# Two-layer graph attention: weighting gathered neighbour rows on ScalarE, summing a batch of them with one VectorE reduction, and another order of the work around it

## The chip, the cores and the metric

One Trainium2 chip, of which the kernel uses one core. The metric is the device time of one execution in microseconds (us): the median over several runs. A smaller number is better.

## What is computed

The input is `x`, 8192 nodes by 256 features, and `adj`, an 8192 x 8192 matrix of 0 and 1 with about 0.1% of ones (symmetric, with ones on the diagonal). Two attention layers, each added to its input:

```python
def reference(x, adj, L0_gnn_W, L0_gnn_a, L1_gnn_a):
    h = jnp.maximum(_layernorm(x, axis=-1), 0.0)
    x = x + _L0_gnn_ref(h, adj, L0_gnn_W, L0_gnn_a)   # softmax over neighbours of e_left + e_right, times h @ W, leaky relu
    h = jnp.maximum(_layernorm(x, axis=-1), 0.0)
    x = x + _L1_gnn_ref(h, adj, L1_gnn_a)
    return x

def _L1_gnn_ref(h, adj, a):
    h1, h2 = h @ a[:d], h @ a[d:]
    e = jax.nn.leaky_relu(h1 + h2.T, negative_slope=0.01)
    attention = softmax(jnp.where(adj > 0, e, NEG_BIG), axis=1)
    return attention @ h
```

## The kernel before

The kernel runs layer 0 first, as dense matmuls over all 64 tiles of 128 nodes. During it, each node's list of neighbours is decoded, and the nodes of the last 44 tiles are sorted by their number of neighbours. The change touches layer 1 alone, which is the second block of the program (from about 1066 us of the profile on). Layer 1 works on the nodes in two ways at once.

**The dense part** does 20 tiles on TensorE. It goes in NGD = 5 groups of G = 4 tiles, and each group in NC = 16 *chunks* of CB = 4 blocks of 128 keys, so there are C = 80 chunks, numbered n. A chunk is 4 blocks x 4 tiles x 2 parts (positive and negative sum, `Vp` and `Vn`) x 2 halves (a high and a low float16 half of each value) = 64 matmuls of 128x128 on 257 columns (L1639). Chunk n needs two masks:
- ScalarE's `signs` (L1300): four activations of 128x512 write which scores are negative, into one of two buffers `adjn`. For the first or second half of chunk n+1 they wait until TensorE is through that half of chunk n-1 (`unit_used`).
- VectorE's `unpack` (L1456, L1459, every second chunk) spreads adjacency bits into `adjp`; `negatives` (L1473) ands it with the signs, `positives` (L1478) xors. After `positives` TensorE may start the chunk (`pos_ready`).

In the first group (chunks 0 to 15) the values themselves have to be made as well: for each of the 64 key tiles SyncE loads a row tile into one of four `hs` buffers, ScalarE makes the high halves (`high_halves`, L1289, 8 per chunk), VectorE the low halves (`low_halves`, L1438, 8 per chunk), and the buffer is free again. At the end of a group VectorE's `take_sums` and ScalarE's `scale_sums` read the eight PSUM banks, `add_negatives` joins the two sums, and the result is stored.

**The sparse part** does the other 44 tiles by gathering. A tile m of 128 nodes has `slots[m]` neighbour slots (24 for the first tile, 4 for the last, 420 in all, worked out by `slot_counts`). GpSimd issues one indirect DMA for each slot (L1264): 128 rows of 258 float32 from `h_of_layer1` into a buffer `gat`. Slots go in 88 *batches* of 3 to 6 (`BS` = 6 at most; tiles of over 6 slots take several), in a ring of `NBUF` = 4 batch buffers. GpSimd may start batch k when VectorE is through all rows of batch k-4 (L1262). For a batch, ScalarE's `weights(k)` makes two small exponentials `e8` (L1321) and VectorE's `larger(k)` their maximum `w8` (L1515). Then VectorE's `add_row` multiplies a row by its weight and adds it to a running sum in `sacc`: L1531 for a tile's first two slots, L1534 for all others. `join`, `divide` and `add_x1` (L1539, L1544, L1550) finish a tile, 128 x1 rows for it come by a DMA that ScalarE issues (`load_rows`), and GpSimd scatters the finished tile to the output (L1255), five batches later at the earliest.

The order on each engine is written out by hand, per chunk n. `pace` says how many rows are to be added by each chunk: none in the first three (`HEAD` = 3.0), then 7 per chunk in the first group and 5 or 6 per chunk (5.3 on average) in the others. Worked out from the code, the numbers for the chunks are 0, 0, 0, 5, 7, 7, ... and 88 rows by the end of chunk 15. On VectorE rows are dealt out between `unpack`, `negatives`, `positives` and the low halves:

```python
add_rows(q0, cuts[0])            # 1 row
negatives(n, g, c)
add_rows(cuts[0], cuts[1])       # 2 rows
positives(n, c)
if g == 0:
    for j in range(CB):
        low_halves(c * CB + j, j % HS)
add_rows(cuts[1], q1)            # the rest
```

On ScalarE the order in a chunk is: high halves of chunk n, `weights` of the batches that begin up to 3 rows (`LEAD`) past the rows of this chunk, `scale_sums` if a group has ended, and then the signs of chunk n+1.

## Time and profile before

| | |
|---|---|
| median of 3 runs | 1924.2 us (1916.23 to 1925.32) |
| profiled execution, its own time | 1914.35 us |
| its span, first to last instruction | 1912.5 us |
| mean granted TensorE clock | 0.930 of full speed |
| busy share of the span: PE, PEld, DVE, ACT, POOL | 88%, 73%, 63%, 51%, 34% |

All times in the text are on the clock of the profiled execution, from the start of its span. PE is TensorE's matmuls, PEld its weight loads, DVE VectorE, ACT ScalarE, POOL GpSimd, SP SyncE. The busy share of PE overstates it, since matmuls overlap: one is recorded as 270 ns or more, while they follow each other every 111 ns at full clock. Counts of matmuls in a stretch of time therefore say more than busy time. A TensorE clock of 1.00 is 2.4 GHz, 0.50 is 1.2 GHz.

### The profile page before, as it was taken

The numbers are of one execution on the slowest core, as the hardware profiler recorded it, in microseconds if no ns is written. First come the engines' busy times: TensorE is split into PE (matmuls) and PEld (weight loads), VectorE is DVE, ScalarE is ACT, GpSimd is POOL, SyncE is SP. The second block draws the span as 40 slices with busy tenths as digits, with TensorE's granted clock in tenths as the row PEclk, the third lists the DMA queues.
The fourth block names the chain that finished last, engine by engine and source line by source line (L and its number), as shares of the span: only waits on it lengthen the run. The fifth ranks groups of instructions, "written<-read, shape, count | busy, mean of one in ns | idle before, by whom it ended". The sixth has DMA issues, their size and how long they took to land. (4 is left out here: it accounts for less than half of the span.)

```text
span 1912.5 us, 37724 instructions
## 1 busy us (share of the span) xinstructions
PE 1691.5 (88%) x13955; PEld 1391.3 (73%) x13955; DVE 1203.0 (63%) x4595; ACT 973.4 (51%) x1367; POOL 651.6 (34%) x607
## 2 busy tenths in 40 slices
PE   6888999999999999999999397677888888978878
PEld 5646888888888888888888285454666667757657
DVE  7488888988888888674444377652435445435434
ACT  5987665665666556666662375432333233323322
POOL 0000000000000000026665548755656657665562
PEclk9998999999999999999999698877889889979889
DMA  8529998888988889989994534533333333433331
GB/s 287 182 76 386 342 349 325 314 311 321 354 320 326 318 310 331 355 333 378 386 379 104 130 94 134 160 80 88 101 89 83 111 89 94 117 100 99 88 92 52
DMA packets 142801, 410.60 MB, mean 215 GB/s; under 512 B 26193, under 2 KB 90066, under 8 KB 109906
## 3 DMA queue, kind: packets, MB, share of 16 engines
q1 hardware_dynamic: 108434, 329.85, 47.6%
q0 software_dynamic: 27904, 73.43, 13.9%
q10 hardware_dynamic: 6336, 5.77, 1.0%
q8 instruction: 62, 1.02, 0.2%
q14 instruction: 65, 0.53, 0.1%
HBM read 368.94 MB, written 40.03 MB: 214 GB/s over the span
## 5 line engine op out<-in xcount | busy, mean ns | idle before, releaser
L984 PE MATMUL banks<-HV,adjT 128*128 128x257 f16 x8192 | 938.8, 274 | 16.7 <-DVE adjT L658 8.8
L984 PEld LDWEIGHTS banks<-HV,adjT 128*128 128x128 fp8e4 x8192 | 792.5, 98 | 148.2 <-DVE HV L688 23.7
L1639 PE MATMUL banks<-Vp,adjp 128*128 128x257 f16 x2560 | 540.6, 292 | 115.4 <-issue 59.2
L1639 PE MATMUL banks<-Vn,adjn 128*128 128x257 f16 x2560 | 538.1, 291 | 48.9 <-issue 47.7
L1264 POOL DMA_INDIRECT gat<-h_of_layer,rec x420 | 465.8, 1109 | 275.5 <-issue 117.9
L444 ACT ACTIVATE adj_f<-adj_i 128x2048 fp8e4<-128x2048 int32 x256 | 480.1, 1898 | 6.6 <-DMA adj_i<-in_adj 6.5
L1300 ACT ACTIVATE adjn<-h1bc,nh 128x512 fp8e5<-128x512 f32 x320 | 212.1, 716 | 446.2 <-remote 272.1
L1639 PEld LDWEIGHTS banks<-Vp,adjp 128*128 128x128 fp8e4 x2560 | 261.2, 103 | 192.3 <-issue 126.5
L1639 PEld LDWEIGHTS banks<-Vn,adjn 128*128 128x128 fp8e4 x2560 | 262.2, 103 | 124.8 <-issue 76.5
L425 POOL DMA_DIRECT2D HV<-x_after_layer x44 | 25.5, 580 | 773.4 <-DVE rank L911 741.3
L1473 DVE TENSOR_TENSOR adjn<-adjp,adjn 128x1024 uint16<-128x1024 uint16 x80 | 55.4, 692 | 334.8 <-ACT adjn L1300 296.0
L1534 DVE SCALAR_TENSOR_TENSOR sacc<-gat,w,sacc 128x257 f32<-128x257 f32 x332 | 152.5, 477 | 0.0
L492 ACT ACTIVATE pk<-banks 128x512 uint16<-128x512 uint16 x64 | 37.9, 593 | 170.3 <-PE banks L969 143.9
L695 DVE RECIPROCAL rden<-banks 128x1 f32<-128x1 f32 x64 | 10.7, 168 | 145.9 <-PE banks L984 115.3
L655 DVE TENSOR_SCALAR adjT<-pk 128x512 uint16<-128x512 uint16 x448 | 94.6, 282 | 0.0
L957 PE MATMUL banks<-w_sb,hT 128*128 128x257 f32 x256 | 68.9, 392 | 15.6 <-ACT hT L456 15.3
L627 DVE SCALAR_TENSOR_TENSOR fold<-adj_f 128x1024 int32<-128x1024 int32 x64 | 77.2, 1206 | 7.4 <-ACT adj_f L444 7.4
L418 POOL DMA_INDIRECT x_after_layer_sorted<-HV,rank x44 | 66.5, 1512 | 13.4 <-issue 12.2
L525 ACT ACTIVATE hh<-x,nmr,rstd 128x256 f32<-128x256 f32 x64 | 38.4, 601 | 53.6 <-DVE nmr L727 45.8
L1515 DVE TENSOR_TENSOR w<-e 128x5 f32<-128x5 f32 (+2 forms) x88 | 13.9, 157 | 77.8 <-ACT e L1321 58.5
L519 ACT ACTIVATE std<-mv,eps 128x1 f32<-128x1 f32 x64 | 18.8, 294 | 86.0 <-DVE mv L719 83.9
L1255 POOL DMA_INDIRECT out<-sout,rec x44 | 46.5, 1058 | 43.1 <-DVE sout L1550 31.8
(158 smaller groups left out, 1395.2 us busy)
## 6 DMA issues: line engine op xcount, KB each, us to landing
adj_i<-in_adj SPq DMA_DIRECT2D x256, 1024.0 KB
h_of_layer<-hh SPq DMA_DIRECT2D x64, 129.0 KB
hs<-h_of_layer SPq DMA_DIRECT2D x64, 129.0 KB
xt<-in_x SPq DMA_DIRECT2D x64, 128.0 KB
packed_adj<-pk SPq DMA_DIRECT2D x64, 128.0 KB
x_after_layer<-x SPq DMA_DIRECT2D x64, 128.0 KB
HV<-in_x SPq DMA_DIRECT2D x14, 512.0 KB, 8.8
gat<-h_of_layer,rec POOLq DMA_INDIRECT x420
```

Of the source, the lines that this page charges most:

```text
L418: pool.indirect_dma_start(x1s_d, bass.IndirectOffsetOnAxis(ap=rank[:, m:m + 1], axis=0), HV[:, T + m % SH, 0:D], None).then_inc(xs_out[m % ...
L444: nc.scalar.activation(adj_f[:, b, q * QC:(q + 1) * QC], adj_i[:, q, :], ACT.Copy, scale=2.0, saturate=False).then_inc(conv_done, 1)
L627: nc.vector.scalar_tensor_tensor(four, whole[:, 0:4 * GW], 1, whole[:, 4 * GW:8 * GW], ALU.logical_shift_right, ALU.bitwise_or)\
L655: last = nc.vector.tensor_scalar(adjT[:, b, i, :], pk[:, pb, :], PAIR << i, 6 - i, ALU.bitwise_and, ALU.logical_shift_left)
L957: last = nc.tensor.matmul(wps[t % 3][:, 0:DV], hT[:, t % 2, c, :], w_sb[:, c, :], start=(c == 0), stop=(c == 1))
L984: last = nc.tensor.matmul(acc[b][:, 0:DV], adjT_h[:, b, i, q, :, h], V0[:, jb, s, 0:DV], start=(jb == 0 and s == 0), stop=(jb == T - 1 and ...
L1255: pool.indirect_dma_start(out, bass.IndirectOffsetOnAxis(ap=rec[:, m, OWN:OWN + 1], axis=0), sout[:, m % NOUT, :], None).then_inc(so_out[m ...
L1264: pool.indirect_dma_start(gat[:, k % NBUF, s - s0, :], None, h_d, bass.IndirectOffsetOnAxis(ap=rec[:, m, s:s + 1], axis=0))\
L1300: i = nc.scalar.activation(adjn_b[:, c % 2, jb // 2, :, jb % 2], h1bc[:, g2, :], ACT.Relu, scale=-BIG, bias=nh2[:, tiles[j]:tiles[j] + 1], ...
L1473: nc.vector.tensor_tensor(part, both, part, ALU.bitwise_and).then_inc(neg_ready, 1)
L1534: nc.vector.scalar_tensor_tensor(acc, x, w, acc, ALU.mult, ALU.add)\
L1639: mm = nc.tensor.matmul(bank[2 * i + part][:, 0:DV], m[:, i * P:(i + 1) * P], V[:, j, s, 0:DV], start=(j == 0 and s == 0), stop=(j == T - ...
```

## The change

Rows of a batch are no longer multiplied and added one by one on VectorE. ScalarE's new `scale_rows(k)` multiplies each row of batch k by its weight in place (one activation of 128x257 per slot), and VectorE's new `sum_rows(k)` sums all of them with one reduction over the slot axis. If a tile has several batches, the sum of one is written into a spare seventh slot of the next batch's buffer and is summed there with the rest. `join` is gone, and `sacc` holds one sum for a tile instead of two.

The steps of a batch are spread over three chunks: for the batches `taken(n)`, `weights` is on ScalarE in chunk n, `larger` on VectorE and `scale_rows` on ScalarE in chunk n+1, `sum_rows` on VectorE in chunk n+2, and `divide` and `add_x1` in the chunk after it. A batch's buffer is handed back to GpSimd after `sum_rows`. `load_rows` is issued by `scale_rows` at a tile's first batch.

In a chunk ScalarE makes the signs of the next chunk first and then does `scale_rows`, the high halves of chunk n+2, and `weights`. VectorE does `negatives` and `positives` next to each other, then `take_sums` where a group has ended, the low halves of chunk n+1, `sum_rows`, `unpack` for the next chunk, and `larger`. The halves of chunk 0, and the high halves of chunk 1, are made ahead of the loop.

The pace is another: worked out from the new constants, one batch is taken in chunk 0 already, 19 batches by the end of chunk 15, then about one per chunk (5.0 rows), 86 of the 88 by the end of chunk 79 (in four chunks none, in ten of them two). The last two batches, of 5 and 4 rows, come behind the last group's `take_sums` and `add_negatives`.

```diff
@@ -1034,8 +1034,9 @@
         BS = 6
         NBUF = 4
         LEAD = 3
-        FIRST = 1.35
-        HEAD = 3.0
+        FIRST = 1.13
+        HEAD = -2.0
+        TAIL = 1.4
         OUT_LAG = 5
         NOUT = 4
 
@@ -1045,28 +1046,16 @@
             parts = -(-slots[m] // BS)
             for i in range(parts):
                 batch.append((m, slots[m] * i // parts, slots[m] * (i + 1) // parts))
...
         at = [sum(slots[:m]) for m in range(NS + 1)]
         last = [max(k for k in range(len(batch)) if batch[k][0] == m) for m in range(NS)]
         fills = [sum(batch[i][2] - batch[i][1] for i in range(k % NBUF, k + 1, NBUF)) for k in range(len(batch))]
         pace = [max(0.0, FIRST * min(n, NC) + max(0, n - NC) - HEAD) for n in range(C)]
...
+        rows_in = [at[NS] * a / (pace[-1] + TAIL) for a in pace]
+        weighed = [0] + [sum(1 for m, s0, s1 in batch if at[m] + s1 <= a) for a in rows_in]
+
+        def taken(n):
+
+            return range(weighed[n], weighed[n + 1]) if n >= 0 else range(0)
...
-            gat = sb("gat", [P, NBUF, BS, ROW], f32)
-            sacc = sb("sacc", [P, 2, 2, DV], f32)
+            gat = sb("gat", [P, NBUF, BS + 1, ROW], f32)
+            sacc = sb("sacc", [P, 2, DV], f32)
...
-            sacc_ready = sem("sacc_ready")
-            row_added = sem("row_added")
+            scaled = sem("scaled")
+            summed = sem("summed")
...
-                        pool.wait_ge(row_added, begin[k - NBUF + 1])
+                        pool.wait_ge(summed, k - NBUF + 1)
...
+                def scale_rows(k):
+
+                    m, s0, s1 = batch[k]
+                    if s0 == 0:
+                        load_rows(m)
+                    act.wait_ge(w8_ready, k + 1)
+                    for i in range(s1 - s0):
+                        x = gat[:, k % NBUF, i, 0:DV]
+                        made = nc.scalar.activation(x, x, ACT.Copy, scale=w8[:, k % 2, i:i + 1])
+                    made.then_inc(scaled, 1)
+
...
-                for m in range(NOUT - 2):
-                    load_rows(m)
+                def high_chunk(c):
+                    for j in range(CB):
+                        high_halves(c * CB + j, j % HS, (c * CB + j) // HS * 16 + 16)
+
+                high_chunk(0)
                 act.wait_ge(nh2_ready, 1)
                 act.wait_ge(h1bc_in[0], 16)
-                act.wait_ge(hb_ready, 2)
                 for h in range(2):
                     signs(h, 0, 0, 0, h, False)
-                weighed = out_done = 0
+                high_chunk(1)
+                act.wait_ge(hb_ready, 2)
                 for n in range(C):
                     g, c = n // NC, n % NC
...
-                    for m in range(out_done, ended(rows_by[n])):
-                        if m + NOUT - 2 < NS:
-                            load_rows(m + NOUT - 2)
-                        out_done = m + 1
-                    for k in range(weighed, lead_of(rows_by[n + 1])):
-                        weights(k)
-                        weighed = k + 1
-                    for m in range(out_done, awaited(rows_by[n + 1])):
-                        if m + NOUT - 2 < NS:
-                            load_rows(m + NOUT - 2)
-                        out_done = m + 1
                     if g > 0 and c == 0:
                         scale_sums(g - 1, g == 1)
                     if n + 1 < C:
@@ -1359,9 +1348,18 @@
                             act.wait_ge(h1bc_in[g1 % 2], 16 * (g1 // 2 + 1))
                         for h in range(2):
                             signs(2 * n + 2 + h, n + 1, g1 % 2, c1, h, 2 * n + 2 + h >= RB)
-                for m in range(out_done + NOUT - 2, NS):
-                    load_rows(m)
+                    for k in taken(n - 1):
+                        scale_rows(k)
+                    if n + 2 < NC:
+                        high_chunk(n + 2)
+                    for k in taken(n):
+                        weights(k)
+                for k in taken(C - 1):
+                    scale_rows(k)
                 scale_sums(NGD - 1, NGD == 1)
+                for k in range(weighed[C], len(batch)):
+                    weights(k)
+                    scale_rows(k)
...
@@ -1511,85 +1509,94 @@
                     b = batch[k][2] - batch[k][1]
                     dve.wait_ge(e8_ready, 2 * k + 2)
                     if k >= 2:
-                        dve.wait_ge(row_added, begin[k - 1])
+                        dve.wait_ge(scaled, k - 1)
                     nc.vector.tensor_tensor(w8[:, k % 2, 0:b], e8[:, k % 2, 0, 0:b], e8[:, k % 2, 1, 0:b],
                                             ALU.max).then_inc(w8_ready, 1)
 
-                def add_row(q):
-
-
-                    m, s, k = row[q]
-                    i = s - batch[k][1]
-                    acc = sacc[:, m % 2, s % 2, :]
-                    if i == 0:
-                        dve.wait_ge(w8_ready, k + 1)
-                    x = gat[:, k % NBUF, i, 0:DV]
-                    w = w8[:, k % 2, i:i + 1]
-                    if s < 2:
-                        if m >= 2 and s == 0:
+                def sum_rows(k):
+
+
+                    m, s0, s1 = batch[k]
+                    b = s1 - s0
+                    dve.wait_ge(scaled, k + 1)
+                    if s0:
+                        dve.wait_ge(summed, k)
+                    if k == last[m]:
+                        if m >= 2:
                             dve.wait_ge(so_ready, m - 1)
-                        nc.vector.tensor_scalar(acc, x, w, None, ALU.mult).then_inc(row_added, 1)
+                        to = sacc[:, m % 2, :]
                     else:
-                        dve.wait_ge(row_added, q - 1)
-                        nc.vector.scalar_tensor_tensor(acc, x, w, acc, ALU.mult, ALU.add)\
-                            .then_inc(row_added, 1)
-
-                def join(m):
-                    dve.wait_ge(row_added, at[m + 1])
-                    nc.vector.tensor_tensor(sacc[:, m % 2, 0, :], sacc[:, m % 2, 0, :], sacc[:, m % 2, 1, :],
-                                            ALU.add).then_inc(sacc_ready, 1)
+                        to = gat[:, (k + 1) % NBUF, batch[k + 1][2] - batch[k + 1][1], 0:DV]
+                    nc.vector.reduce_sum(to, gat[:, k % NBUF, 0:b + (1 if s0 else 0), 0:DV]
+                                         .rearrange("p s c -> p c s"), AX.X).then_inc(summed, 1)
 
                 def divide(m):
-                    dve.wait_ge(sacc_ready, m + 1)
-                    nc.vector.reciprocal(srd[:, m % 2:m % 2 + 1], sacc[:, m % 2, 0, D:DV])\
+                    dve.wait_ge(summed, last[m] + 1)
+                    nc.vector.reciprocal(srd[:, m % 2:m % 2 + 1], sacc[:, m % 2, D:DV])\
                         .then_inc(srd_ready, 1)
 
                 def add_x1(m):
                     dve.wait_ge(srd_ready, m + 1)
                     dve.wait_ge(x1s_in[m % NOUT], 16 * (m // NOUT + 1))
-                    nc.vector.scalar_tensor_tensor(sout[:, m % NOUT, :], sacc[:, m % 2, 0, 0:D],
+                    nc.vector.scalar_tensor_tensor(sout[:, m % NOUT, :], sacc[:, m % 2, 0:D],
                                                    srd[:, m % 2:m % 2 + 1], sout[:, m % NOUT, :],
                                                    ALU.mult, ALU.add).then_inc(so_ready, 1)
 
-                def add_rows(q0, q1):
-
-                    for q in range(q0, q1):
-                        m, s, k = row[q]
-                        for b in range(lead_of(q) if q else 0, lead_of(q + 1)):
-                            larger(b)
-                        add_row(q)
-                        if m and s == 2:
-                            join(m - 1)
-                        if m and s == 3:
-                            divide(m - 1)
-                        if m and s == min(4, slots[m] - 1):
-                            add_x1(m - 1)
-                    if q1 == len(row) and q0 < q1:
-                        join(NS - 1)
-                        divide(NS - 1)
-                        add_x1(NS - 1)
-
+                def low_chunk(c):
+                    for j in range(CB):
+                        low_halves(c * CB + j, j % HS)
+
+                unpack(0, 0, 0, False)
+                low_chunk(0)
                 dve.wait_ge(ab_ready, 1)
+                closing = []
                 for n in range(C):
                     g, c = n // NC, n % NC
-                    q0, q1 = rows_by[n], rows_by[n + 1]
-                    cuts = (min(q0 + 1, q1), min(q0 + 3, q1))
-                    if c % UB == 0:
-                        unpack(n, g, c, n >= 2 * UB)
-                    add_rows(q0, cuts[0])
                     negatives(n, g, c)
-                    add_rows(cuts[0], cuts[1])
                     positives(n, c)
-                    if g == 0:
-                        for j in range(CB):
-                            low_halves(c * CB + j, j % HS)
-                    add_rows(cuts[1], q1)
                     if g > 0 and c == 0:
                         take_sums(g - 1)
+                    for m in closing:
+                        divide(m)
+                    if n + 1 < NC:
+                        low_chunk(n + 1)
+                    for m in closing:
+                        add_x1(m)
+                    closing = []
+                    for k in taken(n - 2):
+                        sum_rows(k)
+                        closing += [m for m in range(NS) if last[m] == k]
+                    if n + 1 < C and (n + 1) % UB == 0:
+                        unpack(n + 1, (n + 1) // NC, (n + 1) % NC, n + 1 >= 2 * UB)
                     if g > 0 and c == 1:
                         add_negatives(g - 1)
+                    for k in taken(n - 1):
+                        larger(k)
+                for m in closing:
+                    divide(m)
+                    add_x1(m)
+                for k in taken(C - 2):
+                    sum_rows(k)
+                    for m in range(NS):
+                        if last[m] == k:
+                            divide(m)
+                            add_x1(m)
+                for k in taken(C - 1):
+                    larger(k)
+                    sum_rows(k)
+                    for m in range(NS):
+                        if last[m] == k:
+                            divide(m)
+                            add_x1(m)
                 take_sums(NGD - 1)
                 add_negatives(NGD - 1)
+                for k in range(weighed[C], len(batch)):
+                    larger(k)
+                    sum_rows(k)
+                    for m in range(NS):
+                        if last[m] == k:
+                            divide(m)
+                            add_x1(m)
...
```

## Rows read from the trace of the kernel before

**Rows 1.** The page's costliest groups: xcount | busy us, mean ns | idle before, releasers.

```profile
L1639 PE MATMUL banks<-Vp,adjp 128*128 128x257 f16 x2560 | 540.6, 292 | 115.4 <-issue 59.2
L1264 POOL DMA_INDIRECT gat<-h_of_layer,rec x420 | 465.8, 1109 | 275.5 <-issue 117.9
L1300 ACT ACTIVATE adjn<-h1bc,nh 128x512 fp8e5<-128x512 f32 x320 | 212.1, 716 | 446.2 <-remote 272.1
L1534 DVE SCALAR_TENSOR_TENSOR sacc<-gat,w,sacc 128x257 f32<-128x257 f32 x332 | 152.5, 477 | 0.0
```

**Rows 2.** Stretches: us; busy (x) of PE, PEld, DVE, ACT, POOL; clock, DMA share, GB/s.

```profile
1081.90:1104.10 22.20, 11.93 (x64) 7.83 (x65) 7.73 (x20) 8.23 (x19) 13.10 (x13) 0.65 0.78 130
...
1140.80:1219.70 78.90, 60.33 (x449) 47.69 (x450) 55.21 (x150) 43.78 (x102) 64.51 (x48) 0.85 0.48 132
1219.70:1271.10 51.40, 28.01 (x193) 19.68 (x194) 27.05 (x79) 16.64 (x41) 29.07 (x29) 0.75 0.43 124
...
1320.00:1868.20 548.20, 466.74 (x3586) 362.51 (x3584) 242.80 (x709) 176.73 (x360) 335.10 (x314) 0.88 0.35 96
1868.20:1903.80 35.60, 35.60 (x322) 30.88 (x319) 17.64 (x50) 10.51 (x20) 7.81 (x8) 1.00 0.16 49
```

**Rows 3.** Shorter stretches, cut where GpSimd's runs of gathers begin, last on or end.

```profile
1403.00:1411.80 8.80, 8.80 (x81) 7.39 (x79) 4.69 (x14) 2.55 (x6) 6.96 (x7) 1.00 0.39 106
1411.80:1418.60 6.80, 3.62 (x26) 2.24 (x24) 0.00 (x0) 0.50 (x1) 5.26 (x6) 1.00 0.49 136
...
1482.80:1490.70 7.90, 7.90 (x65) 6.51 (x64) 3.31 (x12) 2.94 (x6) 6.38 (x6) 0.87 0.59 173
...
1567.50:1589.80 22.30, 22.30 (x203) 19.46 (x202) 12.43 (x37) 7.83 (x16) 18.00 (x15) 1.00 0.43 120
...
1287.50:1315.90 28.40, 14.46 (x59) 5.58 (x57) 4.83 (x15) 3.06 (x6) 22.00 (x22) 0.61 0.38 100
```

**Rows 4.** The waits: who waited for whom, us in total, times, longest.

```profile
POOL gat L1264 <- DVE sacc L1534: 115.8, 25, 22.9
POOL gat L1264 <- DVE sacc L1531: 41.8, 10, 14.7
...
ACT e L1321 <- DMA gat<-h_of_layer,rec: 37.9, 9, 10.9
```

**Rows 5.** The timeline: start us, us, instruction, [idle before <- releaser].

```profile
1123.19 0.48 DVE L1438 SCALAR_TENSOR_TENSOR Vp<-hs,Es,Vp 128x258 f16<-128x258 f32 x1
1123.59 0.48 DVE L1438 SCALAR_TENSOR_TENSOR Vn<-hs,Es,Vn 128x258 f16<-128x258 f32 x1
...
1124.39 3.28 POOL L1264 DMA_INDIRECT gat<-h_of_layer,rec  x1 [0.30 <-issue]
...
1412.63 0.95 POOL L1264 DMA_INDIRECT gat<-h_of_layer,rec  x1 [0.30 <-issue]
```

**Rows 6.** Groups by line, of the operations that the change removes, adds or moves.

```profile
L1289 ACT ACTIVATE Vp<-hs,Es 128x258 f16<-128x258 f32 x64 | 31.8, 497 | 2.7 <-DMA hs<-h_of_layer 2.7
L1438 DVE SCALAR_TENSOR_TENSOR Vp<-hs,Es,Vp 128x258 f16<-128x258 f32 x64 | 30.6, 479 | 0.0
L1531 DVE TENSOR_SCALAR sacc<-gat,w 128x257 f32<-128x257 f32 x88 | 30.3, 353 | 0.5 <-DVE w L1515 0.3
...
L1386 DVE TENSOR_REDUCE red_in<-h2all 128x1 f32<-128x64 f32 x1 | 0.2, 207 | 0.0
...
L1389 DVE TENSOR_REDUCE red_in<-x1g 128x1 f32<-128x44 f32 x1 | 0.2, 188 | 0.0
...
L905 DVE TENSOR_REDUCE rsum<-HV 128x44 f32<-128x880 f32 x1 | 1.8, 1771 | 0.0
...
L525 ACT ACTIVATE hh<-x,nmr,rstd 128x256 f32<-128x256 f32 x64 | 38.4, 601 | 53.6 <-DVE nmr L727 45.8 <-issue 7.7
```

**Rows 7.** The timeline of the end.

```profile
1896.02 0.96 POOL L1255 DMA_INDIRECT out<-sout,rec  x1 [2.08 <-DVE sout L1550]
...
1906.42 1.42 DVE L1505 TENSOR_TENSOR x1g<-x1g,hs 128x256 f32<-128x256 f32 x4
```

15 lines of the change are left out of this document (removed).

## The prediction, made before the changed kernel was run

> **What bounds the kernel now.** I read the page first, then the waits, then layer 1 cut into stretches, and last the timeline of GpSimd beside that of TensorE. The change is in layer 1, so only the time from the first matmul of L1639 at 1081.9 us to the last at 1903.8 us can move, and what hangs behind it. The page names TensorE as the busy engine, but 292 ns for one matmul is an overlapped figure [rows 1]. The last stretch gives the true rate: 322 matmuls in 35.6 us at full clock, 0.111 us each, or 7.1 us for a chunk of 64 [rows 2]. Eighty chunks would be 568 us, and they take 821.9 us. The 254 us above that floor are the subject.
>
> I get the number of chunks of a stretch by dividing its matmuls by 64 [rows 2]. Chunk 0 takes 22.2 us. Chunks 1 to 5 fill the 36.7 us up to the next row and are at the floor. Chunks 6 to 12 take 78.9 us, 11.3 each. Chunks 13 to 15 take 51.4 us. Chunks 16 to 18 fill the 48.9 us from 1271.1 to 1320.0. Chunks 19 to 74 take 548.2 us, 9.8 each, and the last five 7.1 each. The excesses are 15, 1, 29, 30, 28 and 152 us.
>
> Two different causes are behind them. In chunks 6 to 12 the sparse part sets the pace. ScalarE has `weights` ahead of the signs of the next chunk and waits there for gathers, 37.9 us in nine waits [rows 4]; TensorE then waits for masks. GpSimd was left idle for 22.9 us before this, the longest wait for L1534 [rows 4], because no row is added before chunk 3.
>
> The other cause costs more. Look at a run of gathers [rows 3]. From 1403.0 to 1411.8 us GpSimd issues 7 operations and TensorE does 81 matmuls, full rate. From 1411.8 to 1418.6 us, with GpSimd still issuing, TensorE does 26, or 3.8 per us instead of 9. VectorE does nothing and ScalarE almost nothing there, so TensorE is not held by masks; the page puts its idle time down to "issue" [rows 1]. The worst case has 59 matmuls in 28.4 us beside 22 operations of GpSimd, 22 us lost. A short run, 6 operations from 1482.8 us, leaves TensorE at full rate within the counts. So TensorE loses its supply some 9 us into an unbroken run of gathers and regains it when the run ends. Why, no row says. GpSimd's runs end when its four buffers are full: 157.6 us of waits for VectorE [rows 4]. One gather every 0.95 + 0.30 = 1.25 us [rows 5] and some 5.6 issues per chunk, 314 in 56 chunks [rows 2], are 7.0 us against a floor of 7.1. At full rate GpSimd therefore never pauses, TensorE starves, and the pause comes out of TensorE's time.
>
> **Part one: ScalarE multiplies.** 420 activations of 128x257. The nearest rows are L1289 at 497 ns and L525, which reads and writes float32, at 601 ns [rows 6]. Consecutive ones overlap; L1438 on VectorE, recorded at 0.48 us, starts every 0.40 us [rows 5], and I take 0.40 us for ScalarE too (0.50 as the upper end). Five slots are 2.0 us per chunk. Four signs (716 ns each) [rows 1] are under 2.9 us and the small exponentials 0.6 us. This is 5.5 us of a chunk of 7.1 us or more, behind the signs, so from chunk 16 on it costs nothing. If that cover goes, it is up to 2.5 us per chunk.
>
> **Part two: VectorE sums.** It loses 30.3 + 152.5 us [rows 6, 1] and 44 joins. It gains 88 reductions over 420 slots and 44 carried sums, 464 x 257 = 119,248 elements. L905 reduces across a stride, as the new one does: 1771 ns for 880 elements, 2.01 ns each. The contiguous L1386 and L1389 differ by 19 ns for 20 elements, 0.95 ns each, with some 0.15 us fixed. The ends are 126 and 240 us; I take 240, since only L905 is strided. A batch of 5 takes 2.6 us. VectorE then has 1.4 (masks) + 2.9 + under 1.5 us for the rest, below 7.1; this costs nothing outside the first group and the end.
>
> The Trainium skill (SBUF — State Buffer, section "Door 1: The DMA port swizzle") says that consecutive accesses pay when each leaves a 16-byte line, which a step of 1032 bytes always does. It agrees with L905 against the contiguous pair; by it the reductions are 240 us, without it 126 us, and the forecast moves by the 3 us at the end alone.
>
> **Part three: the first group.** Chunk 0 stays: 24 gathers run from the start as before, so TensorE starves as before until about 1104 us. Then a loop forms between ScalarE and VectorE. From the end D of a VectorE chunk, where `larger` is, ScalarE scales (2.4 us), then makes 8 high halves; VectorE can start the low halves at D + 3.0 and needs 8 x 0.40 = 3.2 us for them, then 1.2 batches of reductions (3.4 us), then half an unpack, `larger` and a closing, 0.6 us. That is 10 us per chunk (8.4 with cheap reductions). GpSimd needs about the same: 5.9 operations at 1.25 us, and one of them is stretched to 3.28 us by the block of low halves [rows 5], in all 9.7 us. VectorE starts chunk 2 at about 1106 us; twelve chunks of 10 and two of 8 us put the start of chunk 16 at about 1245 us instead of 1271, a gain of 26 us. But of the 51.4 us of chunks 13 to 15, 22 us are a starvation that could come again. I give it one half and take 15 us. The starvation in chunk 18 (22 us) was as long because GpSimd, three batches behind, could go on without a pause. In the new order three batches sit in the pipeline, and GpSimd can only be about one ahead; I halve this one too: 11 us.
>
> **Part four: chunks 19 to 74.** Signs first and a gather's wait behind them: no gain, since masks come in time here already. What may change is GpSimd's share. Its 335.1 us of busy time and 314 gaps of 0.30 us are 429 us, 1.37 us per operation instead of 1.25 [rows 2, 5]: operations stretch beside VectorE's two-input operations. Without 420 row operations I take 1.29 us, 0.4 us less per chunk: 22 us. The bounds are nothing and 95 us (every chunk at 8.1 us, if each buffer handed back singly gives a pause).
>
> The Trainium skill (SBUF — State Buffer, "Who interferes with whom") has it that a VectorE instruction with two SBUF inputs contends with GpSimd's reads and that a reduction never contends. The trace agrees as far as the 3.28 us gather under the low halves goes; a block of reductions beside gathers is in no row.
>
> **Part five: the end.** The last five chunks were free of gathers and ran at 7.1 us; now gathers go on to chunk 78, at 9.4 us each: 11 us lost. After the last matmul the old order ends with L1505 at 1907.8 us and a store, 4.7 us more [rows 7]. The new one then has two batches in series: `larger` 0.15, scaling 2.1, sum 2.6, closing 0.6, then 0.15, 1.7, 2.1 and 0.6 us, a scatter of 0.96 us and its landing. This ends about 1922 us against 1912.5; with cheap reductions 1919. I take 9 us lost. Moving `load_rows` (44 DMAs on ScalarE's queue) behind the signs costs nothing unless its wait for a scatter bites; GpSimd issues this after the batch that follows. It could add 1 or 2 us in each of the last six tiles.
>
> **The sum.** -15 - 11 - 22 + 11 + 9 = -28 us. From the profiled execution's own 1914.4 us (span 1912.5) that gives 1886 us. This execution lies 10 us under the median of the three runs; on the median, 1924 - 28 = 1896 us.
>
> **Rivals.**
> *A, the forecast:* shorter first group, slightly shorter middle, longer end; 1870 to 1912 us. Chance 0.44.
> *B, the pauses cure the starvation.* VectorE hands back one buffer at one point of a chunk. If even 1 us of pause is enough (the short run speaks for it) [rows 3], chunks 19 to 79 take 8.1 to 8.5 us: 80 to 100 us gained there, less 9 at the end, 15 from the first group: about 1820 us. Against it: buffers came back about one per chunk before as well. Chance 0.15.
> *C, the supply is conserved.* If every gather costs TensorE a fixed number of matmuls wherever it stands, 464 issues cost the same, and only idle masks in the first group are saved, 12 us, against 9 at the end: 1921 us. For it: 254 us over 464 issues is 0.55 us each, and neither number changes. Chance 0.20.
> *D, slower: gathers come faster and starve TensorE more.* One mechanism: VectorE's row operations slow GpSimd down, and where they do TensorE keeps its rate: 15 operations in 22.3 us, 1.5 us each, and 203 matmuls, without loss [rows 3]. Without them every run goes at 1.25 us and starves TensorE from its ninth us. With 0.5 us more lost per chunk in 61 chunks this is +30 us, and with the end's 9, the first group's gain of 15: about 1948 us. It decides from 0.3 us more per chunk on. Chance 0.21.
>
> **How the numbers follow.** The likeliest is A, 1896 us. The median's own runs spread by 0.5%, and under that nothing can be told from no change. A gives faster but for a sliver (0.41), B faster (0.15), C mostly the same (0.18), D slower: 0.58 faster, 0.20 the same, 0.22 slower. A's own range is 1870 to 1912 us. For 8 in 10 I leave out the far side of B and D's tail: 1830 to 1945 us.
>
> **What would show it.** In the new profile: reductions of 2.6 us for 5 slots (1.4 would be the cheap price); the start of chunk 16 near 1245 us; runs of GpSimd that are rarely over two batches; chunks of the middle near 9.4 us; scaling activations starting every 0.40 us; 14 us or more from the last matmul to the end. The prediction is wrong if TensorE starves in short runs as well, if ScalarE waits in `load_rows` or for `larger` and the signs come late, or if chunks of the first group take over 11 us.

## The result, and the profile after

The changed kernel took 1991.7 us (median of 4 runs, 1987.3 to 2001.3) against 1924.8 us (4 runs, 1916.2 to 1933.8): 1.0354 times the time, interval 1.0309 to 1.0398. It is slower, and outside the range of the forecast.

The page of the profile after, the costliest groups that answer to [rows 1, 6]:

```profile
L1646 PE MATMUL banks<-Vp,adjp 128*128 128x257 f16 x2560 | 546.5, 293 | 142.9 <-issue 83.0
L1253 POOL DMA_INDIRECT gat<-h_of_layer,rec x420 | 421.8, 1004 | 417.5 <-DVE gat L1530 159.7
```

The new operations, by line and shape:

```profile
L1321 ACT ACTIVATE gat<-gat,w 128x257 f32<-128x257 f32 x420 | 175.6, 496 | 36.1 <-DVE w L1513 28.7
```
```profile
L1530 DVE TENSOR_REDUCE gat<-gat 128x257 f32<-128x1285 f32 x14 | 34.0, 2431 | 0.7 <-ACT gat L1321 0.6
L1530 DVE TENSOR_REDUCE gat<-gat 128x257 f32<-128x771 f32 x5 | 5.1, 1028 | 0.0
```

A gather became 105 ns shorter (1109 to 1004 ns), yet GpSimd's idle time before gathers grew from 275.5 to 417.5 us, and TensorE's idle time put down to "issue" before this half of its matmuls from 59.2 [rows 1] to 83.0 us. The waits of the kernel after, which answer to [rows 4]:

```profile
PEld banks L1646 <- issue: 283.8, 284, 15.7
...
POOL gat L1253 <- DVE gat L1530: 159.7, 25, 18.0
...
POOL gat L1253 <- DVE sacc L1530: 129.0, 20, 18.6
```

GpSimd now waits 288.7 us in 45 waits for a buffer to be handed back, where it was 157.6 us in 35. ScalarE's wait for gathers fell from 37.9 to 7.4 us, as meant. The stretches of layer 1, with columns as in [rows 2]: first group, the four other groups, the end:

```profile
1083.00:1262.20 179.20, 134.08 (x1024) 105.19 (x1025) 126.08 (x232) 129.42 (x305) 98.03 (x94) 0.86 0.48 124
1262.20:1969.20 707.00, 553.89 (x4096) 416.56 (x4096) 327.31 (x511) 327.31 (x727) 354.14 (x358) 0.84 0.30 84
1969.20:1992.40 23.20, 0.24 (x3) 0.00 (x0) 9.55 (x21) 6.14 (x17) 1.92 (x2) 0.57 0.15 48
```

The kernel before, cut at the same points (start of chunk 16, last matmul):

```profile
1271.10:1903.60 632.50, 535.82 (x4096) 413.65 (x4096) 276.46 (x806) 198.45 (x403) 377.99 (x355) 0.87 0.34 93
```

So the first matmul comes 1 us later, the first group is 10 us shorter (179 for 189), the 64 chunks of groups 1 to 4 take 74.5 us more (707.0 for 632.5, 11.0 us a chunk for 9.9), and the end 14 us more (23.2 for 8.9): 80 us, the difference of the spans 1992.4 and 1912.5. The place is the middle. There I took every pair of matmuls whose starts lie more than 0.35 us apart, and summed what each such gap has beyond the usual 0.11 us: 202 us in 228 gaps after, 131 us in 165 before. So 71 of the 74.5 us are such gaps. None of them ends with a mask that came late: 193 us of the 202 are put down to "issue" or to nothing (120 of the 131 before), the rest to the sums of a finished group being taken out of the banks.

One of them, cut where GpSimd's run of gathers begins, where TensorE falls, where it recovers and where the next run begins:

```profile
1568.70:1576.40 7.70, 7.70 (x72) 6.69 (x70) 5.09 (x8) 3.72 (x9) 5.82 (x7) 1.00 0.32 88
1576.40:1584.40 8.00, 3.46 (x16) 1.41 (x14) 0.00 (x0) 1.34 (x2) 4.77 (x5) 0.72 0.37 98
1584.40:1590.80 6.40, 6.39 (x48) 5.17 (x48) 4.68 (x7) 4.95 (x11) 0.04 (x1) 0.82 0.08 24
1590.80:1597.10 6.30, 6.30 (x59) 5.50 (x58) 4.10 (x7) 4.13 (x10) 5.07 (x5) 1.00 0.45 125
1598.20:1606.50 8.30, 6.85 (x59) 5.19 (x56) 4.60 (x7) 4.49 (x11) 5.24 (x6) 1.00 0.48 128
```

The reader is to see the fall from 72 matmuls in 7.7 us to 16 in 8.0, with VectorE at nothing and ScalarE nearly so, and GpSimd at work for the first 6 us of it. The run had 11 operations. The recovery is not at full rate at once: the granted clock is 0.82 of the upper level (2.4 GHz) after TensorE idled, and 48 matmuls take 6.4 us. A run of five operations from 1590.8 us, behind a pause of 8.4 us, costs nothing. The next one, also of five and behind a pause of 1.1 us (last row), costs 2 us.

Counted over groups 1 to 4, with a run ended by any pause over 0.6 us: before, the 11 runs of up to six operations cost nothing. After, there are 17 such runs. The ten behind a pause of over 2 us cost nothing, and of the seven behind a shorter one six cost something, 13.5 us together. In runs of nine operations or more the first gap comes at a median of 8.0 us from the run's start, where it was 10.4 us before. The runs of seven or more cost 0.64 us of such gaps for each operation of GpSimd (179 us, 280 operations), where it was 0.34 (97 us, 282 operations).

Not only new matmuls are late. ScalarE's signs wait for TensorE to be through half a chunk, and the page can't name what released 251.8 us of these waits ("remote"). From the records of the instructions: of 124 such halves in groups 1 to 4, ScalarE, idle, began its signs over 1 us after TensorE's last matmul of the half in 41, up to 18.5 us after it. The end of the first group shows it on VectorE, whose `take_sums` waits for the last matmul of the group alone:

```profile
ACT adjn L1289 <- remote: 251.8, 41, 19.6
```
```profile
1250.27 0.39 PE L1646 MATMUL banks<-Vn,adjn 128*128 128x257 f16 x2
...
1260.63 0.16 DVE L1480 TENSOR_TENSOR cnt<-idf,banks 128x8 f32<-128x8 f32 x1 [12.92 <-remote]
```

Ten us lie between the two, and GpSimd's run of gathers ends at 1258.5 us, in between. VectorE, in contrast, follows ScalarE's signs within 0.5 us in all 64 chunks. So during a long run two things come late, TensorE's next matmuls and the word that those already started are done. A matmul that has started isn't waiting for its instruction, so a theory of the cause has to explain more than a lack of those.

### The profile page after: what moved, and what is told of

It reads as the page before. It is cut to its first block and busy times, and to the rows that moved or that the text cites. A ratio compares the mean times of both kernels' runs of the same rounds, so it can differ in the third digit from the quotient of the medians.

```text
span 1992.4 us, 37734 instructions
## 1 busy us (share of the span) xinstructions
PE 1707.7 (86%) x13955; PEld 1393.4 (70%) x13955; DVE 1268.8 (64%) x4219; ACT 1139.8 (57%) x1787; POOL 598.5 (30%) x607
## 5 line engine op out<-in xcount | busy, mean ns | idle before, releaser
L1646 PE MATMUL banks<-Vp,adjp 128*128 128x257 f16 x2560 | 546.5, 293 | 142.9 <-issue 83.0
L1646 PE MATMUL banks<-Vn,adjn 128*128 128x257 f16 x2560 | 544.8, 293 | 70.8 <-issue 69.5
L1253 POOL DMA_INDIRECT gat<-h_of_layer,rec x420 | 421.8, 1004 | 417.5 <-DVE gat L1530 159.7
L1289 ACT ACTIVATE adjn<-h1bc,nh 128x512 fp8e5<-128x512 f32 x320 | 211.0, 715 | 359.3 <-remote 251.8
L1321 ACT ACTIVATE gat<-gat,w 128x257 f32<-128x257 f32 x420 | 175.6, 496 | 36.1 <-DVE w L1513 28.7
L1530 DVE TENSOR_REDUCE sacc<-gat 128x257 f32<-128x1542 f32 (+3 forms) x44 | 128.4, 2918 | 24.5 <-ACT gat L1321 18.6
L1530 DVE TENSOR_REDUCE gat<-gat 128x257 f32<-128x1028 f32 (+4 forms) x44 | 98.5, 2238 | 2.9 <-ACT gat L1321 2.4
L957 PEld LDWEIGHTS banks<-w_sb,hT 128*128 128x128 f32 x256 | 45.3, 197 | 23.4 <-ACT hT L456 19.6
```

Of the source, the lines that this page charges most:

```text
L957: last = nc.tensor.matmul(wps[t % 3][:, 0:DV], hT[:, t % 2, c, :], w_sb[:, c, :], start=(c == 0), stop=(c == 1))
L1253: pool.indirect_dma_start(gat[:, k % NBUF, s - s0, :], None, h_d, bass.IndirectOffsetOnAxis(ap=rec[:, m, s:s + 1], axis=0))\
L1289: i = nc.scalar.activation(adjn_b[:, c % 2, jb // 2, :, jb % 2], h1bc[:, g2, :], ACT.Relu, scale=-BIG, bias=nh2[:, tiles[j]:tiles[j] + 1], ...
L1321: made = nc.scalar.activation(x, x, ACT.Copy, scale=w8[:, k % 2, i:i + 1])
L1530: nc.vector.reduce_sum(to, gat[:, k % NBUF, 0:b + (1 if s0 else 0), 0:DV] .rearrange("p s c -> p c s"), AX.X).then_inc(summed, 1)
L1646: mm = nc.tensor.matmul(bank[2 * i + part][:, 0:DV], m[:, i * P:(i + 1) * P], V[:, j, s, 0:DV], start=(j == 0 and s == 0), stop=(j == T - ...
```

## The same kernel in two conditions

The experiments ran in five more sessions, each with the kernel before beside them. In one its median was 1933.7 us (13 runs, 1921.6 to 1942.3), close to the result's 1924.8. In the other four it was 1754.9, 1753.6, 1753.4 and 1758.5 us. The difference sits in layer 1: its first matmul starts at 1081.9 us in the one trace of this kernel and at 1082.6 in the other. A session kept its condition through all its runs, and one chip showed both. What chooses the condition no row says, and I could not bring it about; it stays open. I call the 1930 us condition *starved* and the other *supplied*. Times I compare only inside a session. For stretches of traces that isn't possible everywhere, since the starved kernel before has its one trace in the session of the result; where two sessions are compared, the text says so.

The kernel before itself, one execution in the supplied condition, over groups 1 to 4 and over 20 us of them:

> The kernel before, unaltered, for a profile beside the two others. Where TensorE isn't starved (near 1754 us): GpSimd without idle time from chunk 3 on and TensorE waiting for masks behind it, 3 to 4 us after the gathers' pace; a change that frees GpSimd of VectorE's two-input operations then gains. Where it is: the same stretches as in the first profile, within 2%.

```profile
1241.30:1738.70 497.40, 464.82 (x4095) 399.03 (x4096) 280.44 (x806) 198.56 (x403) 377.23 (x356) 0.98 0.42 119
```
```profile
1400.00:1420.00 20.00, 20.00 (x183) 17.46 (x181) 12.27 (x37) 8.47 (x18) 15.43 (x16) 1.00 0.58 173
```

It took 1749.3 us. Sixteen operations of GpSimd in 20 us without a pause leave TensorE at 183 matmuls, the full rate. GpSimd is the bound here: beyond the 0.30 us between two operations it is idle for 13 us in 497, ScalarE waits 252.2 us for gathers instead of 37.9 [rows 4], and the chain that ended last has gathers for 20% of the span. The same gathers go with a starved TensorE in one condition and not in the other: no gap of over 0.35 us between matmuls is put down to "issue" here, and ScalarE's signs begin over 1 us after TensorE's half once in 124 halves, 1.6 us late.

The page's queue of instructions is the same in both conditions, the changed kernel starved and the kernel before supplied:

```profile
q8 instruction: 62, 1.02, 0.2%
```

Its transfers in layer 1, 48 in each trace, take 1.05 us on the mean in both. Once under way they are not slower. Whether they are asked for or begun late no row says, but the short loop below settles that they are not the cause.

## The experiments

Three theories stood. *Rival D* (theory 1 in the texts on record): gathers no longer slowed by VectorE's two-input operations starve TensorE more. *The new order and pace* (theory 2): one hand-back point per chunk, three batches in a pipeline of four buffers, so that GpSimd's pauses fall badly, whoever does the arithmetic. *Code*: TensorE's loop over a group is unrolled, and its instructions come too late. Against all of them stood the conserved supply (C).

**Starved session** (kernel before 1933.7 us). First the changed kernel unaltered.

> The changed kernel, unaltered, as a control: the kernel before ran at 1754.9 us on the chip of the first four experiments, against 1924.8 us where the change was measured, and its changed form was not among them. If this chip is like that one (before near 1755 us): theory 1 (the loss of the change is starvation of TensorE beside gathers, which that chip does not show) expects 1735 to 1745 us, faster than before; theory 2 (order and pace cost by themselves) expects over 1800 us. If this chip is like the one of the result (before near 1925 us): 1985 to 2000 us.

1995.6 us (4 runs, 1981.9 to 2017.6; without the longest the median is 1993.5), ratio 1.028 (1.022 to 1.034). The slowdown repeats; groups 1 to 4 took 704.9 us, 0.3% from the result's trace.

**Row arithmetic back on VectorE,** in the new order and at the new pace:

```
-                    act.wait_ge(w8_ready, k + 1)
-                    for i in range(s1 - s0):
-                        x = gat[:, k % NBUF, i, 0:DV]
-                        made = nc.scalar.activation(x, x, ACT.Copy, scale=w8[:, k % 2, i:i + 1])
-                    made.then_inc(scaled, 1)
...
-                    nc.vector.reduce_sum(to, gat[:, k % NBUF, 0:b + (1 if s0 else 0), 0:DV]
-                                         .rearrange("p s c -> p c s"), AX.X).then_inc(summed, 1)
...
+                            nc.vector.scalar_tensor_tensor(acc, x, w, acc, ALU.mult, ALU.add)\
+                                .then_inc(row_added, 1)
```

> The changed kernel's order and pace with the row operations back on VectorE. On a chip like that of the result, theory 1 expects 1915 to 1945 us and gathers of 1.1 us on average, theory 2 1975 to 2000 us. On a chip like that of the first experiments: 1730 to 1742 us again.

1936.4 us (10 runs, 1926.6 to 1957.1), ratio 1.001 (0.998 to 1.005). First group, and groups 1 to 4:

```profile
1082.10:1231.40 149.30, 124.96 (x1024) 101.64 (x1025) 113.24 (x300) 94.22 (x216) 110.47 (x84) 0.92 0.55 139
1231.40:1925.20 693.80, 554.47 (x4095) 418.87 (x4096) 291.61 (x809) 199.76 (x404) 383.86 (x367) 0.84 0.32 87
```

This is where theory 1 had put it (1915 to 1945 us, gathers of 1.1 us; a gather took 1094 ns on the mean), and not theory 2 (1975 to 2000 us). By the medians of the starved session the order and pace alone cost nothing that can be told from zero, and the arithmetic costs 59 us (1995.6 against 1936.4).

The traces say where, with less certainty. From this kernel to the changed one of the same session the arithmetic adds 30 us in the first group (149.3 to 179.4), 11 in groups 1 to 4 and 4 at the end. The order and pace have to be read across two sessions: against the trace of before they shorten the first group by 40 us (189.2 to 149.3), lengthen groups 1 to 4 by 61 (632.5 to 693.8) and the end by 10 (8.9 to 19.1), 32 us in all where the medians have 3. The other 29 us are the choice of executions: the trace of before lay 10 us under its median, this one 10 above its own, and the two sessions' medians of the kernel before differ by 9. Where these lie no trace says. If all of them lay in groups 1 to 4, the order and pace would cost some 32 us there and the arithmetic some 23. So of the loss in that stage 32 to 61 us belong to the order and pace and 11 to 23 to the arithmetic.

The mechanism of rival D is to be seen in these traces. The time per operation of GpSimd, gap included, falls from 1.346 to 1.288 us between the two. The first gap in runs of nine or more comes at a median of 10.7 us with the rows on VectorE, as before the change (10.4), and at 8.0 us with the reductions, in both traces of the changed kernel. The gaps between matmuls grow from 184 to 199 us. What the order and pace add is another thing: a median onset as late as before, and yet 0.50 us of gaps for each operation in runs of seven or more, for 0.34 (0.59 in the changed kernel run beside it).

**Short loop**: TensorE's inner loop runs over 4 chunks, so that the code of a group is 12 chunks long instead of 16 (the value tiles of chunks 0 to 3 are used again in it).

```
+                    chunks(g, False, range(4))
+                    with pe.Fori(1, NC // 4 - 1) as r:
+                        chunks(g, False, range(4), r)
+                    chunks(g, False, range(NC - 4, NC))
```

> The changed kernel with the shorter TensorE program (an inner loop over four chunks in groups 1 to 4, the value tiles of chunks 0 to 3 used in it). On a chip like that of the result: under 1940 us if TensorE starves for its own instructions, 1980 to 2000 us if for something else. On a chip like that of the first experiments: within 3 us of the changed kernel, since nothing starves there.

1996.9 us (4 runs, 1990.6 to 2011.5), ratio 1.032 (1.026 to 1.038), the same as the changed kernel; gaps between matmuls 200 us. The trace says more than the time. Its instruction queue on the page, and 535 us of it:

```profile
q8 instruction: 30, 0.49, 0.1%
```
```profile
1435.00:1970.00 535.00, 423.06 (x3090) 314.46 (x3089) 249.82 (x404) 247.70 (x557) 270.33 (x272) 0.83 0.30 83
```

The queue moved 30 packets for 62, and in these 535 us none at all (32 in the same 535 us of the changed kernel, with its 16 chunks of code; the page's other queue of instructions, q14, moved 12 in both). Yet 151 us of them are gaps between matmuls. So TensorE starves as much while this queue moves nothing, and late transfers of its code are refuted as the cause.

**Supplied sessions.** These four came first, on one chip (before 1754.9 us): the gathers left out (the buffers are filled once), the rows on VectorE, a filling of 256 float32 on GpSimd awaited behind each gather, and the short loop.

```
+                nc.gpsimd.memset(gat[:, :, :, :], 0.5).then_inc(gat_set, 1)
...
-                        pool.indirect_dma_start(
```
```
+                        nc.gpsimd.memset(idle[:, 0:256], 0.0).then_inc(idled, 1)
+                        pool.wait_ge(idled, at[m] + s + 1)
```

> The changed kernel without its 420 gathers: the gather buffers are filled once with a constant, so the rows of the sparse part are not the reference's; everything else, the 420 scaling activations and 88 reductions among it, stays. Theory 1 (TensorE is starved while gathers run): chunks at 7.1 us from chunk 16 on, no gaps of about 1 us between matmuls, and a time near 1720 us. Theory 3 (ScalarE's and VectorE's new work, or the order of the engines, slows TensorE by itself): gaps and chunks over 9 us stay, and the time stays over 1850 us.

> The changed kernel's order and pace, but a batch's rows are multiplied and added one by one on VectorE as before, in the place of the reduction, and ScalarE's 420 activations are gone. Theory 1 (VectorE's row operations slowed the gathers down and so protected TensorE): gathers are back at a mean of 1.1 us, and the time falls to 1915 to 1945 us. Theory 2 (the order and the pace are the loss: buffers given back in another rhythm, gathers up to the last chunk): the time stays at 1975 to 2000 us.

> The changed kernel with a GpSimd memset of 256 float32 and a wait for its end behind every gather, so that gathers start every 1.6 to 1.8 us instead of every 1.25 us. Theory 1: TensorE starves less; chunks of the middle go to 8.5 to 9.5 us, bounded by GpSimd itself, and the time falls below 1960 us although GpSimd does more. Theory 2: GpSimd has 150 us more to do, and the time rises above 2000 us.

> The changed kernel with a shorter TensorE program: in groups 1 to 4 chunks 4 to 11 are two turns of one inner loop of four chunks, so that a group's code is 12 chunks long instead of 16. In the inner loop the value tiles are those of chunks 0 to 3, so the dense part's sums are not the reference's; the number and shapes of matmuls are the same. If TensorE starves because its own instructions have to be fetched while gathers run, the loss falls in groups 1 to 4, by a third or all of it: under 1940 us. If what starves it is something else (the memory ports, the masks' semaphores), the time stays at 1980 to 2000 us.

They took 1724.1 (ratio 0.983), 1736.7 (0.989, 0.985 to 0.992), 1835.5 (1.047, 1.044 to 1.049) and 1739.2 us (0.992). None can speak on starvation, since there was none to cure. The spaced gathers show only that GpSimd's time is the path here: in groups 1 to 4 it waits 0.8 us for a buffer in all, its other 99 us of idle time are short waits, most of them for the fillings, and the stage takes 548 us where the changed kernel takes 467. Repeated in another session (before 1753.6), the first and the third gave the same, 1723.6 (0.983) and 1835.4 us (1.047):

> The changed kernel without its 420 gathers (constant rows instead, so the sparse part's output is not the reference's), on another chip. If the gathers are the whole difference between the chips: 1724 us as on the first chip, and no gaps between matmuls beyond those at the group ends. If TensorE is starved here by something else as well: over 1750 us.

> The changed kernel with a small memset and a wait for it behind every gather, on another chip. Where TensorE starves: theory B expects less starvation, since gathers are 1.6 us apart instead of 1.25: groups 1 to 4 under 680 us; if only the number of gathers counts, they stay at 706 us or rise, since GpSimd has 150 us more to do. Where nothing starves: 1832 to 1836 us again.

**Depth of the ring**, in the same session: the changed kernel with five buffers (two semaphores of the setup merged to have one more), and the kernel before with three.

```
-        NBUF = 4
+        NBUF = 5
```

> The changed kernel with five gather buffers instead of four. Theory A (a batch now keeps its buffer over three chunks, so GpSimd is stopped for long after every starvation and the depth of the ring is what the new order lacks): groups 1 to 4 fall from 706 us towards 650 us, and the time to 1930 to 1960 us where the kernel before takes 1925 to 1935 us. Theory B (TensorE is starved by the number and the rate of gathers, whatever the ring): within 10 us of 1995 us. Where nothing starves (before near 1755 us) both expect 1735 to 1745 us.

> The kernel before with three gather buffers instead of four. Theory A: slower by 30 us or more, like the new order, because the ring is one buffer shorter. Theory B: within 10 us of the kernel before in groups 1 to 4; the first group may lose some, since GpSimd is the bound there.

1730.5 us (ratio 0.988, 0.985 to 0.990) and 1771.1 us (1.011, 1.008 to 1.013). **The changed kernel** again, with both beside it, in the next session (before 1753.4):

> The changed kernel as it is. Where the kernel before takes near 1755 us: 1735 to 1745 us by theory 1 (the change is faster where TensorE isn't starved). Where it takes near 1930 us: 1985 to 2005 us again.

> The changed kernel with five gather buffers. On a chip that starves TensorE: theory A (the new order lacks ring depth) 1930 to 1960 us; theory B (number and rate of gathers) within 10 us of the changed kernel. On one that doesn't: 1730 us again.

> The kernel before with three gather buffers. On a chip that starves TensorE: theory A slower by 30 us or more, theory B within 10 us in groups 1 to 4. On one that doesn't: 1771 us again.

> The changed kernel without its gathers. On a chip that starves TensorE: 1724 us if the gathers are the whole difference between the chips, over 1750 us if something else starves TensorE too. On one that doesn't: 1724 us.

1740.4 us (5 runs, ratio 0.993, 0.991 to 0.995), 1732.1 (0.989, 0.986 to 0.992), 1770.6 (1.010, 1.007 to 1.014) and 1723.3 us (0.984). The changed kernel's groups 1 to 4, and its last gathers after the last matmul:

```profile
1238.30:1705.10 466.80, 456.80 (x4096) 396.76 (x4096) 322.41 (x505) 323.79 (x725) 352.12 (x353) 1.00 0.45 125
...
1705.10:1740.20 35.10, 0.23 (x3) 0.00 (x0) 15.95 (x28) 8.37 (x23) 12.01 (x13) 0.56 0.26 79
```

The same kernel that is 3% slower in the starved condition is 0.7% faster in this one. Groups 1 to 4 take 467 us for 497 before (one trace each, in sessions that differ by 5 us on the kernel before). GpSimd is the bound, and an operation of it costs 1.299 us for 1.360, which over some 355 operations is 22 of the 30 us; with the rows on VectorE the stage took 483 us, at 1.36 us an operation. The first group gives 6 us, and the end takes 26 back, because 12 operations of GpSimd start after the last matmul. Five buffers are the best kernel that ran, 8 us under the changed one in the same session and 9 us above the one without gathers. A last session (before 1758.5) confirmed it: 1733.3 us (0.986, 0.984 to 0.988) beside 1725.5 us without gathers (0.981).

> The changed kernel with five gather buffers. Where TensorE is starved beside gathers: theory A (the new order lacks ring depth) 1930 to 1960 us; theory B (number and rate of gathers) within 10 us of 1993 us, the changed kernel's time there. Where it isn't: 1731 us again.

> The changed kernel without its gathers. Where TensorE is starved: 1724 us if the gathers are the whole difference, over 1750 us if something else starves TensorE too. Where it isn't: 1724 us.

The five buffers and the kernel without gathers were meant for the starved condition above all, and each session they ran in was supplied. So two things were not tested where they matter: that the starvation goes when the gathers go, and that deeper buffering gives back what the new order costs there.

## Why the prediction was wrong

The step that failed is part four, chunks 19 to 74, and with it the choice of A over D: it took time that GpSimd saves as time that TensorE gets back, -22 us for its 56 chunks. The 64 chunks of groups 1 to 4 took 74.5 us more instead, since TensorE starves by the run, and faster gathers starve it sooner in a run. Point by point:

**Part one, right.** An activation of `scale_rows` is recorded at 496 ns, and five in a row take 2.10 us, so they start every 0.40 us. From chunk 16 on they lie behind the signs.

**Part two, right.** A reduction of 5 slots took 2.43 us (forecast 2.6; the cheap price was 1.4); all 88 take 226.9 us for 119,248 elements, 1.90 ns each (forecast 240 us). The price of L905 holds, with one exception: the five reductions over 3 slots took 1028 ns, 1.33 ns an element at the same stride. The Trainium skill (SBUF — State Buffer, "Door 1: The DMA port swizzle") has it that each access which goes over to a new 16-byte line costs extra. The reductions over 4 to 7 slots, 1.9 to 2.0 ns an element, agree with this; those over 3 slots pay much less, and no run here shows why.

**Part three, the ring right, the starvation not.** Chunks 3 to 14 took 10.5 us each for a forecast 10 (1116.2 to 1241.7 us). But from the start of chunk 15 to that of chunk 16 it took 20.5 us, 11.8 of them the late end of the group shown above, and chunk 17 took 23.3 us: the starvation came again where I had counted half. The start of chunk 16 was forecast at 1245 us from the ring alone and 1256 with the half; it was 1262.2. Of the forecast 15 us, 9 came. The ring between ScalarE and VectorE is dear: with the rows on VectorE the first group is 30 us shorter in the starved condition and 13 us (139.4 for 152.8, two sessions) in the supplied one.

**Part four, wrong in sign.** Its term of 0.4 us less of GpSimd per chunk is exact: an operation with its gap fell from 1.366 to 1.289 us, by 5.6 issues 0.43 us. The Trainium skill's rule behind it (SBUF — State Buffer, "Who interferes with whom") is that a VectorE instruction with two SBUF inputs contends with a GpSimd instruction that reads SBUF, and that a reduction never does. The traces agree with it, in the supplied condition too (1.360 to 1.299 us). But in the starved condition GpSimd's time is not what is paid for. The runs became shorter, the long ones mostly two batches and 13 to 16 us, and cost more: 0.71 us of TensorE for each operation of GpSimd in groups 1 to 4 (707.0 less 64 x 7.1, over 358), against 0.50 before and 0.65 with the rows on VectorE. Runs up to six operations cost nothing behind a long pause (0.6 us at most in the repeat), as the prediction had read from [rows 3], but behind a pause of under 2 us most of them do: its own sign of being wrong, starvation in short runs, came true there. GpSimd's idle time in that stage, beyond the 0.30 us between operations, went 149, 200, 245 us (before, rows on VectorE, after). In place of 9.4 us a chunk stood 11.0. The forecast for groups 1 to 4, 632.5 - 11 - 22 + 11 = 610.5 us, missed by 96 us, and the rest by 12.

**Part five, mis-sized.** The end was forecast 9 us longer and was 14. The timeline of the end has the term that I left out. The last matmul starts at 1969.2 us, and VectorE turns to `larger` here:

```profile
1973.34 0.16 DVE L1513 TENSOR_TENSOR w<-e 128x5 f32<-128x5 f32 x1
```

`larger` of the first of the two batches waits 3.9 us behind the sums of the last group on VectorE (L1480 from 1969.48 us, to L1503). After the last scatter 7.8 us pass to the end of the span; the forecast's terms leave some 7 for that. The two batches in series are as forecast.

**The rivals.** B is refuted: there were more pauses and more starvation, and pauses of 1.1 us did not protect the run behind them. C is refuted too: 462 of the 464 indirect DMAs of GpSimd start before the last matmul, where it was all of them, and it took 80 us more. D has the sign, and its mechanism is there: TensorE falls 2.4 us sooner in a run. In groups 1 to 4 it carries 11 to 23 us of the 74.5; its 1948 us is 44 too low. By the medians of one session the arithmetic costs 59 us in all, but half of that is the ring of the first group, and the order and pace, which D takes as harmless, cost 32 to 61 us in groups 1 to 4. Inside the order and pace I did not separate the depth of the ring, the signs ahead of `weights`, and the rows spread over the whole of the time. This stays open, as does why TensorE starves at all.

## What to carry to other kernels

Run the kernel before beside each version in the same session and look at its absolute time: here the verdict on one change turns from 3.5% slower to 0.7% faster with a condition that the kernel does not choose. When a stage is added to a pipeline, count how many batches are held between its stages; here a fifth buffer was worth 8 us in the supplied condition. And cut an edit into its order and its arithmetic before pricing either. Totals that agree (1936.4 and 1933.7 us) can hide a gain of some 40 us in one stage and a loss of 32 to 61 in the next; but when a trace lies 10 us off its median, what it gives to a stage is no surer than that.

## What the runs showed of the hardware

- One kernel, unchanged, takes 1754 us in some sessions and 1930 us in others on the same chip. Groups 1 to 4 of the kernel before differ by 135 us (497.4 and 632.5, one trace each); 96 of them are gaps over 0.35 us between matmuls (35 us in 17 gaps against 131 in 165), and the granted clock is lower, 0.87 of the upper level on the mean of the stage against 0.98.
- In the starved condition TensorE falls into gaps at a median of 8.0 us into an unbroken run of GpSimd's indirect DMAs when VectorE reduces, 10.4 to 10.7 us when it multiplies and adds rows, and recovers some 2 us past the run's end. In the supplied condition runs without any pause cost it nothing. That the gathers are the cause is argued from this timing; removing them was never tried in the starved condition.
- What is late then is also TensorE's word that matmuls are done: 41 of 124 waits of ScalarE for it ended over 1 us after the last matmul concerned, up to 18.5 us, against none in the supplied trace of the same kernel. VectorE followed ScalarE within 0.5 us throughout.
- It is not the fetching of TensorE's code: in the short loop's trace 151 us of gaps fall into 535 us in which the page's queue of instructions moves no packet.
- A gather's recorded time depends on what VectorE does: 1109 ns on the mean beside multiply-and-add over rows (1094 in the new order), 1004 ns beside reductions.
- A reduction across a stride of 1032 bytes costs 1.9 to 2.0 ns an element over 4 to 7 slots and 1.33 over 3.
